# Splitting the low-rank and router weights of the first batch right behind its layer norm, and planning the weight pairs in five groups

## What is computed

```python
q1 = fake_quant(layernorm(x), x1_scale, x1_zp)
q2 = fake_quant(ctx, x2_scale, x2_zp)
x = x + matmul(q1, q2)
n = layernorm(x)
probs = softmax(n @ W_router.T)
topk_p, topk_i = top_k(probs, 2)
w = scatter(topk_i, topk_p / sum(topk_p))
h = einsum('td,erd->ter', n, lora_A)
lora = einsum('ter,eor,te->to', h, lora_B, w) * 2.0
out = x + n @ W_base.T + b_base + lora
```

## Time and profile before

| | |
|---|---|
| median of 3 runs (lowest, highest) | 1007.65 us (1007.12, 1008.27) |
| the profiled execution: its time, its span | 1010.88 us, 1008.8 us |
| mean granted TensorE clock | 0.985 of full speed |
| instructions | 12927 |
| DMA traffic | 198.65 MB |

### The profile page before, as it was taken

How to read it: one execution, slowest core, us unless ns; L and a number is a source line. 1 busy time by engine, 2 the same in 40 slices (tenths; PEclk the granted TensorE clock), 3 DMA queues, 4 the chain that set the end, 5 groups by cost and what they waited for, 6 DMA issues and landing times.

```text
span 1008.8 us, 12927 instructions
## 1 busy us (share of the span) xinstructions
PE 938.0 (93%) x4518; PEld 439.0 (44%) x4518; DVE 590.8 (59%) x705; ACT 496.6 (49%) x479; POOL 361.7 (36%) x270
## 2 busy tenths in 40 slices
PE   1899999889778998989999899998999999999998
PEld 1754444344334444444434344443444444444443
DVE  6798745958887673647878687207434243252251
ACT  5756665646756466464656666213432242233230
POOL 3332216946533254634234142103243243143240
PEclk9999999979989999999999999999999999999999
DMA  9999897858750596847577594991252352351421
GB/s 349 368 352 398 335 345 258 297 176 251 278 168 22 185 243 233 244 154 227 166 234 211 183 281 141 364 379 37 84 131 31 101 130 31 100 131 27 146 43 42
DMA packets 61733, 198.65 MB, mean 197 GB/s; under 512 B 5728, under 2 KB 22240, under 8 KB 53088
## 3 DMA queue, kind: packets, MB, share of 16 engines
q1 hardware_dynamic: 56048, 177.30, 48.1%
q0 software_dynamic: 5616, 20.45, 12.3%
HBM read 138.49 MB, written 56.62 MB: 193 GB/s over the span
## 4 chain that ended last, share of the span: by engine, by line
PE 43%; DVE 9%; DMA 8%; issue 5%; ACT 4%; POOL 2%; SPq 0%; ACTq 0%; DVEq 0%; POOLq 0%
PE PS L916 12%; PE PS L918 12%; PE PS L917 12%; DVE S L668 4%; DMA S<-centred_dram 3%; DMA Braw<-in_bT_dram 2%; DVE S L667 1%; DMA centred_dram<-S 1%; DMA yops_dram<-S 1%; DMA S<-in_wT_dram 1%; PE PS L939 1%; PE PS L937 1%; PE PS L938 1%; PE PS L1073 1%; DVE S L600 1%
## 5 line engine op out<-in xcount | busy, mean ns | idle before, releaser
L882 POOL TENSOR_TENSOR Q<-S,Q 128x1024 f16<-128x1024 f32 x49 | 106.5, 2180 | 141.8 <-ACT Q L877 141.8
L877 ACT ACTIVATE Q<-S 128x1024 f16<-128x1024 f32 x74 | 76.3, 1049 | 115.3 <-DVE S L861 115.1
L916 PE MATMUL PS<-XA,Q 128*128 128x512 f16 x336 | 128.4, 382 | 0.1
L917 PE MATMUL PS<-XA,Q 128*128 128x512 f16 x336 | 128.0, 381 | 0.0
L918 PE MATMUL PS<-XA,Q 128*128 128x512 f16 x336 | 128.0, 381 | 0.0
L490 PE MATMUL PS<-Q,S 128*128 128x512 bf16 x512 | 116.9, 390 | 10.2 <-ACT S L438 8.2
L490 PE MATMUL PS<-EX,S 128*128 128x512 bf16 (+1 forms) x544 | 107.4, 358 | 2.7 <-ACT EX L404 2.7
L844 ACT ACTIVATE S<-S,WC 128x1024 f32<-128x1024 f32 x64 | 71.4, 1139 | 76.3 <-DMA S<-in_wT_dram 62.8
L916 PE MATMUL PS<-EX,Q 128*128 128x512 f16 x256 | 97.3, 380 | 6.0 <-DVE S L966 3.3
L861 DVE TENSOR_TENSOR S<-S 128x1024 f32<-128x1024 f32 x64 | 93.8, 1466 | 8.4 <-ACT S L844 4.4
L551 POOL TENSOR_TENSOR S<-S 128x1024 f32<-128x1024 f32 x33 | 84.1, 2561 | 39.7 <-ACT S L607 21.5
(11 more groups left out here) (221 smaller groups left out, 1519.1 us busy)
## 6 DMA issues: line engine op xcount, KB each, us to landing
S<-in_cT_dram SPq DMA_DIRECT2D x32, 1024.0 KB, 8.4
S<-in_wT_dram SPq DMA_DIRECT2D x32, 1024.0 KB, 5.6
EX<-in_xn_dram SPq DMA_DIRECT2D x24, 512.0 KB, 7.2
yops_dram<-S SPq DMA_DIRECT2D x48, 256.0 KB, 4.0
out_dram<-Q POOLq DMA_DIRECT2D x23, 512.0 KB, 5.4
S<-out_dram SPq DMA_DIRECT2D x17, 512.0 KB, 4.4
XA<-in_xT_dram SPq DMA_DIRECT2D x16, 512.0 KB, 9.4
out_dram<-XA SPq DMA_DIRECT2D x16, 512.0 KB, 9.2
```

The lines of the kernel that those rows point to most:

```text
L877: tok["hi", n] = s, free, src, act.do(w + free, lambda e: e.activation(ring[s][:, 0:1024], src, ACT.Copy, bias=0.0, scale=1.0))
L882: l = line.do([h] + free, lambda e: e.tensor_tensor(ring[s][:, 1024:2048], src, ring[s][:, 0:1024], ALU.subtract))
L916: e.matmul(bank(bk), wh[:, c], yh(op, k), start=(fresh and k == 0), stop=False, skip_group_check=not fresh)
L917: e.matmul(bank(bk), wh[:, c], yl(op, k), start=False, stop=False, skip_group_check=not fresh)
```

## The change

*Weights of batch 0.* The early copy of A in EX stays and is the source of the split; there is no second load of A for batch 0. The high part goes to `a_hi0` (a buffer of the squares, S 10752), the low part to ring slot 1. `a_prep(0)` stands at us(-47.5) instead of us(-1.3) and `r_prep` at us(-45.72) instead of us(-0.3), both behind operand step 0. The router's split weights go to `gd` first and are copied by one ScalarE instruction (`r_keep`, us(9.07)) to where they stood before, for batch 1. Operand steps 6 and 7 wait for the split of A, as they write over it. Both halves of pair 0's weights are loaded together at us(-17.88). The ring of weight slots begins at slot 2.

*Groups.* `stage_of` sorts the pairs into five groups: pair 0, pairs 1 to 3, pairs 4 to 7, pair 8, pairs 9 to 15. All weight work, `post`, `store`, `y_on`, `first_on`, `lo_on` and `w_sum` take their times and engines by group.

*The plan.* Nearly every entry of `V` has another value. In the shortened diff stand those that the text below speaks of.

```diff
-    "l_turn": (9.76, 15.19, 17.65, 18.93, 29.74, 30.41, 36.57, 41.98),
+    "l_turn": (10.75, 8.85, 19.87, 19.33, 28.6, 30.94, 35.69, 41.98),
-    "l_xn": (-0.52, 1, 2.5, 2.87, 12.3, 12.37, 17, 17.7), "l_ctx": (2.71, 4, 16.84),
+    "l_xn": (-19.72, 1.16, 4.65, 4.92, 7.98, 15.24, 18.7, 19.4), "l_ctx": (2.48, 10.53, 17.12),
-    "conv_on": "ppddpdaaddppaaaaapppdaddadpapaaa",
+    "conv_on": "dpdppddapapdpaaapapppadaadappaaa",
-    "square": 3.75, "square_on": "mdpppppppppppppd",
+    "square": 2.76, "square_on": "pdpppdppdpppdpdd",
-    "add1_on": "pppddpmppmppppmp", "lt_on": "dddpddddpdpdddpd",
+    "add1_on": "ddpddpmpmmppdpmm", "lt_on": "dddpddpdddddddpd",
-    "sq1_on": "pmpmpdpppppdppdp", "norm1": 40.01, "norm1_step": 6.14,
+    "sq1_on": "dmpppdpdpppddppp", "norm1": 36, "norm1_step": 6.4,
-    "ops1_step": 19.6, "ops1_in": (7.2, 0.41, -0.53, 4.83, 5.8, 7.28, 7.49, 0.86),
+    "ops1_step": 19.0, "ops1_in": (5.95, 1.14, 1.97, 4.76, 1.12, 4.26, 7.49, 0.7),
-    "w_norm": ((-24.41, -22.37, -22.19, -21.91), (-15.09, -22.61, -18.06, -14.26)),
+    "w_norm": ((-23.43, -22.37, -22.19, -21.94), (-14.18, -22.61, -17.85, -18.32), (-17.16, -15.37, -17.31, -17.92)),
-    "lo_on": ("pdpddpp", "pdpppdp"),
+    "lo_on": ("ddpddpp", "ddpddpp", "ddpdddp", "ddppppd", "pdpdddp"),
...
+    a_early, a_hi0 = cut(EX, 10240, 2048), cut(S, 10752, 1024, F16)
-    r_a = cut(Q, 7168, 256, F16).rearrange("p (k m) -> p k m", k=KT)
-    r_b = cut(Q, 7424, 256, F16).rearrange("p (k m) -> p k m", k=KT)
+    r_mem = [gd, cut(Q, 7168, 512)]
...
-            wh = [[], [], [once["a_read"]], [once["a_read"]]]
+            a_w = once["a_done"] if k >= 6 else [once["a_read"]]
+            wh = [[], [], a_w, a_w]
...
     def a_prep(b):
-        (s, f), (u, g) = take_slot(), take_slot()
-        hi, lo, src = ring[s], ring[u], raw[0]
+        if b:
+            (s, f), (u, g) = take_slot(), take_slot()
+            hi, lo, src, came, slots_ = ring[s], ring[u], raw[0], raw_in[0], [s, u]
+        else:
+            assert (1, 7) in front and u8_free[2] is not None and ring_free[1] == []
+            hi, lo, src, came, slots_ = a_hi0, ring[1], a_early, once["a_early"], [1]
+            f, g = misc["b_free"], u8_free[2] + misc["acc_read"]
...
     def r_prep():
-        z = [pool.do([once["q_done"]], lambda e: e.memset(r_a, 0.0)), pool.do([once["q_done"]], lambda e: e.memset(r_b, 0.0))]
+        r_a, r_b = r_ab[0]
+        w = misc["acc_read"]
+        z = [pool.do(w, lambda e: e.memset(r_a, 0.0)), pool.do(w, lambda e: e.memset(r_b, 0.0))]
...
+    def r_keep():
+        once["r", 1] = [act.do([once["q_done"]] + once["r", 0], lambda e: e.activation(r_mem[1], r_mem[0], ACT.Copy, bias=0.0, scale=1.0))]
...
+    stage_of = lambda i: 0 if i == 0 else 1 if i < 4 else 2 if i < 8 else 3 if i == 8 else 4
...
-        s1 = gd
-        wt_ = [block_done[7, "t", 3]] if b else []
+        s1 = gd if b else ob[3][:, 0:512]
+        wt_ = [block_done[7, "t", 3]] if b else [once["q_done"]]
...
     def first_raw():
         raw_free[0], raw_free[1] = list(ctx_free[0]), list(ctx_free[1])
-        raw_load("A", (0,))
-        raw_load(0, (1,))
+        raw_load(0)
     def first_ring():
         ring_free[0] = sum(u8_free, []) + misc["acc_read"]
-        ring_free[1] = list(ring_free[0])
-        a_prep(0)
+        items[0] = 2
...
-    at(us(V["first_ring"] + V["raw0"]), raw_load, 0, (0,))
+    at(us(V["a0"]), a_prep, 0)
+    at(us(V["r0"]), r_prep)
+    at(us(V["r1"]), r_keep)
...
-        c = 0 if i == 0 else 1 if i < 8 else 2 if i == 8 else 3
+        c = stage_of(i)
...
-            at(us(t + u - V["w_sum"][n]), w_sum, i, n)
+            at(us(t + u - V["w_sum"][c][n]), w_sum, i, n)
-            at(us(t + u + 0.8), w_lo, i, n, lines[V["lo_on"][b][n]])
+            at(us(t + u + 0.8), w_lo, i, n, lines[V["lo_on"][c][n]])
-                at(us(t + V["store"][h]), store, i, h)
+                at(us(t + V["store"][c][h]), store, i, h)
-            at(us(t + u + V["post"][b][n]), post, i, n)
+            at(us(t + u + V["post"][c][n]), post, i, n)
```

More of the change, by code:

```diff
@@ L38 @@
[L38 to L48, removed]
@@ new lines @@
+    "l_gemm": (24.07, 35.7, 24.08, 26.31, 33.17, 31.58, 37.36, 44.19, 42.45, 44.88, 45.41, 45.47), "ln1_step": 10.37,
+    "xn_load": -12.64, "ln1_stats": 0.55, "ln1_quant": 5.57, "ln1_turn": 10.52, "ln1_back": 17.08, "back_on": "daaaadad",
+    "add0": 9.83, "mean": 3.66, "centre": 3.05, "centre_step": 2.3, "square": 2.76, "square_on": "pdpppdppdpppdpdd",
+    "add1": 10.67, "sq_end": 4.67, "var_a": 8.49, "var_b": 11.8, "early": (3.97, 4.61, 13.57, 24, 4.03, 18.5, -0.7),
+    "ops0": -54.1, "ops0_step": 8.94, "ops0_in": (3.28, 3.77, 3.47, 1.17, 5.4, -0.7, 3.73, 1.89),
@@ new lines @@
+    "la_on": "pppdpdppdpdddddd", "first_raw": -17.88, "first_ring": 1.06, "a0": -47.5, "r0": -45.72, "r1": 9.07,
+    "norm1": 36, "norm1_step": 6.4, "tile_load": -7.9, "cd_store": 1.32, "yd_store": -2.12, "var1": 4.53, "ops1": 13.4,
+    "ops1_step": 19.0, "ln_load": 4.63, "ops1_in": (5.95, 1.14, 1.97, 4.76, 1.12, 4.26, 7.49, 0.7), "start": 31.96,
+    "pair": 39.04, "a_load": 7.94, "a_prep": 20.06,
+    "router": ((4.44, 1.22, 21.79, 7.32, 14.07, 12.52, 10.87, 20.95, 23.13), (4.15, -16.29, 7.73, 1.41, 9.54, 17.03, 21.21, 13.51, 24.94)),
@@ L659, in y_operands @@
             if k == 0:
+                assert "s_r" in once
                 bank_free[4] = bank_free[5] = None
@@ L750, in b_load @@
     def b_load(j):
-        assert "r" in once
+        assert ("r", 0) in once
         raw_what[2] = j
@@ L765, in early @@
     def early():
[L767 to L768 removed]
+        came = once["a_early"] = sp.do(xn_free[1], sl_c[1], a_early, aT)
         r_in = sp.do([], sl_c[2], rraw, rT)
@@ L805, in a_prep @@
             t += [[h, l]]
-        raw_free[0] = [l]
-        w_at["A", b] = s, u, t
+        if b:
+            raw_free[0] = [l]
+        else:
+            once["a_done"] = [l]
+            ring_free[1] = None
+        w_at["A", b] = hi, lo, slots_, t
     def w_norm(i):
@@ L1075, in mm @@
             return ins
-        w = once["r"] + bank_free[bk] + bank_free[bk + 1] + sum((opr[op, k] for op in (B11, T1, B21, B22) for k in range(8)), [])
+        w = once["r", b] + bank_free[bk] + bank_free[bk + 1] + sum((opr[op, k] for op in (B11, T1, B21, B22) for k in range(8)), [])
         bank_free[bk] = bank_free[bk + 1] = None
```

67 lines of the change are left out of this document (36 added, 31 removed).

## The result

The changed kernel takes **1001.51 us** (median of 7 runs, 997.20 to 1005.78) against 1007.65 (7 runs, 1006.55 to 1009.44): a ratio of 0.9935 with a 95% interval of 0.9910 to 0.9961, which is 6.5 us less (6.1 by the medians). In a second set of runs (e1) the same pair stood at 998.64 and 1010.06, a ratio of 0.9897 (0.9874 to 0.9920). The forecast was 997.7, 9.9 less; its range held both medians. The sum came out, several of its terms did not.

A forecast was written before the change was run, and what follows sets the result against it. TensorE was 93% busy, so only its idle time and slow clock could be won, with VectorE and GpSimd setting its gaps. +1.0 - 5.0 - 2.2 - 1.6 - 1.5 - 0.6 = -9.9 gave 997.7 us, range 988.5 to 1008.5.

The forecast's parts named there:

- rival 2: "Given back": pairs hang on second-batch operand steps, waits return, a longer gap costs 2 us in slow clock; 1003.5 us, chance 0.19.
- A: Start: tile 0's transpose goes behind tile 1's; +1.0 us, bounds a loss of 4.0 and a gain of 2.3.
- dense products beginning after 30 us: At the start: a sign that the prediction is wrong; they began at 28.04 us before.
- B: Variance path, 150 to 220 us: VectorE takes square additions from GpSimd; -5.0 us, bounds 0 and -7.5.
- C: Low-rank and router weights split some 57 us earlier; the second batch's row sum leaves GpSimd; -2.2 us, bounds 0 and -4.7.
- at about 204: Variance path: the closing addition comes at about 204 us, not 209.22, the variance matmul at 205.3, not 210.49.
- started earlier, it only waits there instead: Low-rank product: without the 4.94 us gap it waits before its last eighth, for operand step 7.
- near 307: Low-rank product: a sign that the prediction is right is its end near 307 us instead of 314.2.
- D: Pairs 1 to 3: scale steps and a square addition re-sorted to shorten waits; -1.6 us, bounds -7.4 and +2.9.
- E: Pairs 4 to 7: stores sooner, partial results ahead of the next weight sum; -1.5 us, bounds -7.9 and +4.4.
- F: Second router and rest: logit reduction no longer behind a weight sum; -0.6 of 2.75 us, bounds -2.7 and +2.
- VectorE as a slower bound: 150 to 312 us: VectorE's order, not GpSimd, sets the variance path; about 1013.5 us, chance 0.12.

The follow-up runs named there:

- e1: The changed kernel again, nothing edited: 998.64 us, ratio 0.9897 against the kernel before.
- e5: The kernel before the change again, nothing edited, one execution for a second profile: span 1008.1 us.
- e12: The changed kernel with products that nobody reads put into TensorE's longest waits: 1004.24 us, ratio 0.9962.
- e4: The changed kernel with the order of the first 45 us as before the change: 998.95 us, ratio 0.9890.
- e9: The changed kernel with start, low-rank and router weights, pair 0's plan, first router and some neighbouring times as before: 1002.41 us, ratio 0.9920.
- e6: The kernel before with the change's variance path alone: 1004.62 us, ratio 0.9934.
- e8: The changed kernel with low-rank and router weights split right ahead of operand step 6, not behind step 0: 1000.26 us, ratio 0.9910.
- e2: The changed kernel with one split of the first batch's operand step 6 back from GpSimd on VectorE: 1000.66 us, ratio 0.9911.
- e3: The changed kernel with e2's edit and VectorE's two additions for pair 0's weight norm behind step 7's second multiplication: 1000.03 us, ratio 0.9895.
- e10: The changed kernel with the edits of e3 and e4 together: 1000.92 us, ratio 0.9897.
- e7: The changed kernel with pairs 1 to 7 and the second batch's norm and operand steps planned as before: 1010.85 us, ratio 1.0009.
- e11: The changed kernel with only the weights, evacuations and stores of pairs 1 to 7 planned as before: 1032.73 us, ratio 1.0217.

## Why the prediction was right, step by step

**The total** was right in sign and size: ratios of 0.9935 and 0.9897 against 0.9901. That it came out so near is in good part luck. All six terms are idle time of TensorE, and TensorE's idle time fell by some 2 us only: span less busy time is 70.8 and 68.2 us in the two profiles of before, 68.4 and 66.9 in the two of the changed kernel. What fell, by some 6 us, is TensorE's busy time for the same matmuls. The second profile of either kernel, e5 and e1 (the first ones stand in the earlier trace rows and above):

```profile
PE 939.9 (93%) x4498; PEld 441.0 (44%) x4518; DVE 589.2 (58%) x705; ACT 496.4 (49%) x479; POOL 361.0 (36%) x270
PE 929.2 (93%) x4498; PEld 435.2 (44%) x4518; DVE 601.8 (60%) x725; ACT 505.7 (51%) x492; POOL 287.2 (29%) x238
```

All executions say the same. The 62 of before average 1009.8 us at a mean clock of 0.9837, the 13 of the changed kernel 1000.3 us at 0.9914. If the low clock costs one minus the clock, times the span, that is 16.4 us before and 8.6 after: 8 of the 9.4 us between them (at most, since what a low clock costs can be hidden, as in e12). The prediction named the clock as one of two things that can be won, gave it no term, and priced it in rival 2 alone, at 2 us. Two errors cancelled: the waits of the front moved where the sum has them gone, and the clock gave what they did not. By stretch, in us, with TensorE's idle time in brackets:

| stretch | before, e5 | changed, e1 |
|---|---|---|
| up to the first router | 318.5 (46.5), 317.9 (45.6) | 317.3 (47.8), 315.2 (49.0) |
| from the first to the second | 365.2 (18.2), 363.6 (16.5) | 364.3 (15.6), 358.6 (13.0) |
| from the second to the end | 325.1 (6.1), 326.6 (6.1) | 322.4 (5.0), 322.4 (5.0) |

**A.** +1.0, "because tiles 4 to 7 wait for the same buffers as before": mis-sized where it stands. The first dense product is 2.6 us late (30.64 against 28.04), nearer to the bound of 4.0, and "dense products beginning after 30 us", a sign of being wrong by the prediction, came (30.22 in e1). That the loss is carried to the first router, e4 shows (2.7 us); that it costs time does not show: 998.95 against 998.64.

**B.** -5.0, measured alone -6.7 (4.4 to 8.9): right in size, though not all of it as waits. It is also the one part shown to win by itself: its ratio of 0.9934 is that of the whole change in the first set of runs (0.9935; 0.9897 in the second), and A and C, the structural edit among them, add nothing that shows (e9). It acts as told: GpSimd's queue shortened, VectorE the next bound (its closing addition at 208.18, not 209.22). That it came 1.0 earlier and not 5.2, as "at about 204" had it, is A's late start in part: in e6, with the old start, the matmul behind it comes 4.1 earlier. The term missed the clock, which I had counted only in a rival: from 0.80 and 0.86 to 1.00 between 200 and 225 us in e6. Over e6's 12 executions the mean clock accounts for some 4 of the 6.7 us, worked out as above. In the changed kernel itself that window is at 0.86 in one profile and at 1.00 in the other.

**C.** -2.2 with the reasoning that the end of the operand steps stays: the move as such is worth nothing that shows (e8), as said, and the subtraction beside GpSimd's row sum did get its 2.18 us back (0.69 us at 291.76, where it took 2.87). The step that failed is where the waiting would go: "started earlier, it only waits there instead", before its last eighths. It waits in its middle, for pair 0's scale, which has no term in the sum. The two waits, for the weights and for that scale, were 4.94 and 1.29 us in the first profile of before and 3.88 and none in e5; the changed kernel has none and 5.81, e8 has 5.60 and 1.98. A part of the 5.81 is a split of step 6 that went to GpSimd, a letter of the table that I had not costed. It held up VectorE by 3.44 us but TensorE only by 1.1 (e2), for ScalarE's squares of pair 0's weights are late next (e2, e3). So the low-rank product's last matmul started at 315.01 and 312.92; without that letter at 311.65 (e2), with the additions later and the old start as well at 309.80 (e10), not near 307.

**D, E.** -3.1 together. From the first to the second router the three profiles with the old plan need 365.2, 363.6 and 364.9 us (before, e5, e6), eight with the new one, on whatever front, 358.6 to 365.8, 361.8 on average: -2.8, with ranges that overlap. The waits make -2.3 of it: TensorE is idle for 18.2, 16.5 and 15.1 us of that stretch with the old plan, 13.0 to 15.6 (14.3 on average) with the new one. (Of the 7 us that the prediction read as waits for partial results on VectorE, 1.4 were for ScalarE's scaling, L844.) Pair 1's wait of 2.91 is gone as foretold; a new one of 1.6 and 1.9 us stands at 390 to 392, at pair 2's scale. The undoing could not measure it: e7 and e11 take 371.1 and 391.4 us between the routers, more than either plan.

**F.** -0.6, measured -2.7: mis-sized. From the second router's start to the end it is 325.1 us before and in e6 and 326.6 in e5; with the new order it is 322.4 in seven profiles, the two of the changed kernel among them, and 323.1 to 324.1 in four (e2, e3, e9, e12), 322.9 on average. The wait fell from 2.75 to 1.65, and the clock accounts for the rest. In all three profiles with the old order the window behind that wait is at 0.93, in all eleven with the new one at 1.00; the four longer ones have a window at 0.93 at the second router's first matmuls instead, 675 to 700:

```profile
690.00:715.00 25.00, 22.25 (x100) 10.64 (x99) 13.90 (x30) 9.17 (x10) 5.59 (x3) 0.93 0.23 84
```

```profile
690.00:715.00 25.00, 23.35 (x113) 10.82 (x111) 12.93 (x25) 12.64 (x14) 4.37 (x3) 1.00 0.25 90
```

The first is e6, the second e1. The 1.1 us more of busy time is the shorter wait; that more was done in it shows in the clock beside it.

**Rivals.** VectorE as a slower bound did not come. "Given back" came in part: what A and pair 0's scale cost in the front, and what e3, e4 and e10 won there, does not show in the medians at the end. In the profiles the pairs take up a part as waits: e10, with no low clock there, keeps 1.9 of its 3.1 us. More goes by the clock. Between the routers no 25 us window is at 0.93 in e1, e2, e3 and e10, which need 358.6 to 360.4 us; e8 has one and needs 361.3; the changed kernel's first profile and e9 have two and need 364.3 and 364.0; e4 has four and needs 365.8. So of the 5.7 us between the two executions of one kernel 2.6 are waits and 3.2 are TensorE's busy time (348.8 against 345.6 us) for the same matmuls. Longer scale waits and low clock come together there, and the profiles don't tell which comes first.

**What the clock is worth by itself** stays open: the 8 us above are an account, not an experiment. At a mean clock of 0.988 the two kernels are close, 1003.56 and 1005.78 us against five executions from 1004.26 to 1007.89. That ties the gain to the clock, but a long wait makes both a low clock and a long time; e12, which raised the clock alone, delayed too much to part them.

## What to carry to other kernels

Before a wait is counted as won, ask which wait of the same engine ends next: 4.9 us ahead of the low-rank product went, and 5.8 us stood in its middle. Cost every letter of a re-sorted plan too: one that was left out, a split on another engine, made 1.1 of the 5.8. After the change set busy time beside idle time: here the idle time hardly fell, and the gain was in the clock. When a wait is shortened, look at the clock in the window behind it as well; a wait 1.1 us shorter was worth 2.7 on average where TensorE was the bound, and a stretch at 1.2 GHz cost next to nothing where VectorE was (e12, one execution). A plan whose parts were sorted together can't be measured by putting half of it back.

## What was not expected of the hardware

A wait of 2.75 us was followed by a clock of 0.93 in each of three profiles, one of 1.65 us at the same place by 1.00 in each of eleven. The length of a wait alone does not decide it: ahead of the second router's first matmuls TensorE waits 2.2 to 2.3 us in each of the thirteen profiles without fillings, and the clock fell behind that wait in four of them (e2, e3, e5, e9). The Trainium skill (TensorE: Matmul & The Clock Gate, HAM oscillation) has TensorE restart at half clock after idling, and e12 agrees: with the waits filled the mean clock rose from 0.991 to 0.997. That the low clock can be nearly free where another engine is the bound, e12's front shows: 0.25 us at the first router.
